# Softmax denominators one pair of heads later, in the form of the product with values, and the rotation split in keys and queries: a macaron block on one core

## What is computed

```python
x = x + 0.5 * ffn(layernorm(x))      # 2 shared and 8 routed experts, top 2
x = x + attn(layernorm(x))
x = x + 0.5 * ffn(layernorm(x))
```

```python
q = q * cos + rotate_half(q) * sin + fenc        # the same for k
dots = einsum('bhid,bhjd->bhij', q, k) * scale
attn = softmax(dots, axis=-1)
out = einsum('bhij,bhjd->bhid', attn, v)
return out @ w_out.T + b_out
```

## Time and profile before

| | |
|---|---|
| median of three runs | 1268.65 us (1264.79, 1268.65, 1268.78) |
| profiled execution, its own time | 1265.84 us |
| its span, first to last instruction | 1264.0 us |
| TensorE busy | 1224.8 us, 97% of the span |
| VectorE, GpSimd, ScalarE busy | 958.6, 897.0, 629.8 us |
| mean granted TensorE clock | 0.999 of 2.4 GHz |

### The profile page before, as it was taken

One profiled execution on the slowest core, in us unless ns is written; L12 is line 12 of the kernel. 1 busy time (PEld: TensorE's weight loads), 2 busy tenths in 40 slices (PEclk: granted clock), 3 DMA queues, 4 the chain that ended last, 5 costly groups with the idle time before them and its releaser, 6 DMA issues.

```text
span 1264.0 us, 20948 instructions
## 1 busy us (share of the span) xinstructions
PE 1224.8 (97%) x7346; PEld 777.6 (62%) x7346; DVE 958.6 (76%) x1439; ACT 629.8 (50%) x921; POOL 897.0 (71%) x652
## 2 busy tenths in 40 slices
PE   5999999899999999999999999999999999999998
PEld 3666666456666656565666666665666655666665
DVE  6666687778898888888888888788888766666632
ACT  3444532455555555546555555555555554434422
POOL 0444346688898999898889889889989862543443
PEclk9999999999999999999999999999999999999999
DMA  5351241123232323233332323232323221442140
GB/s 170 135 184 55 81 145 24 34 52 69 57 72 52 77 52 74 54 69 60 64 66 60 68 60 69 52 77 54 73 54 73 56 44 20 142 143 105 47 159 17
DMA packets 118677, 95.35 MB, mean 75 GB/s; under 512 B 75760, under 2 KB 85008, under 8 KB 118320
## 3 DMA queue, kind: packets, MB, share of 16 engines
q1 hardware_dynamic: 118064, 93.75, 30.0%
q10 hardware_dynamic: 512, 0.26, 0.1%
HBM read 57.53 MB, written 2.88 MB: 48 GB/s over the span
## 4 chain that ended last, share of the span: by engine, by line
PE 85%; DVE 6%; issue 4%; ACT 2%; POOL 2%; DMA 1%; SPq 0%; ACTq 0%; DVEq 0%; POOLq 0%
PE banks L1165 17%; PE banks L1144 14%; PE banks L455 12%; PE banks L468 8%; PE banks L1083 7%; PE banks L1003 6%; PE banks L1181 5%; PE banks L1149 4%; PE banks L1190 4%; PE banks L1011 3%; PE banks L1122 1%; DVE side_turned L702 1%; PE banks L410 1%; POOL work L1438 1%; PE banks L417 1%
## 5 line engine op out<-in xcount | busy, mean ns | idle before, releaser
L1015 DVE TENSOR_REDUCE neg_max<-banks 128x2 f32<-128x1024 f32 x256 | 305.3, 1226 | 12.7 <-PE banks L1003 7.7
L1267 ACT ACTIVATE work<-banks 128x1024 f32<-128x1024 f32 x256 | 262.5, 1027 | 92.7 <-PE banks L1149 76.6
L1165 PE MATMUL banks<-work 128*64 128x512 f32 x1024 | 233.8, 598 | 0.0
L1438 POOL TENSOR_TENSOR work<-work 128x1024 f32<-128x1024 f32 x64 | 158.8, 2482 | 74.2 <-PE banks L1165 74.2
L1428 POOL TENSOR_TENSOR turn<-turn,side_turned 128x512 f32<-128x512 f32 x128 | 164.9, 1311 | 30.7 <-DMA side_turned<-side 30.7
L1422 POOL TENSOR_TENSOR turn<-turn,fenc 128x512 f32<-128x512 f32 x128 | 163.3, 1298 | 2.0 <-DVE side L1338 2.0
L1433 POOL TENSOR_TENSOR qk_l<-turn,qk_h 128x512 fp32r<-128x512 f32 x128 | 162.1, 1289 | 2.1 <-ACT qk_h L992 2.1
L1165 PEld LDWEIGHTS banks<-work 128*64 128x64 f32 x1024 | 67.8, 136 | 132.7 <-issue 110.0
L1359 DVE TENSOR_TENSOR work<-work 128x1024 f32<-128x1024 f32 x64 | 107.4, 1677 | 37.7 <-PE banks L1165 37.5
L816 POOL TENSOR_TENSOR o_raw<-o_raw,work 128x512 f32<-128x512 f32 x52 | 67.2, 1293 | 88.0 <-DVE o_raw L734 80.7
L816 POOL TENSOR_TENSOR work<-work 128x512 f32<-128x512 f32 x44 | 56.6, 1297 | 96.0 <-DVE work L734 49.6
(11 more groups left out here) (178 smaller groups left out, 2454.7 us busy)
## 6 DMA issues: line engine op xcount, KB each, us to landing
work<-share SPq DMA_DIRECT2D x32, 1024.0 KB, 9.4
side_turned<-side SPq DMA_DIRECT2D x256, 128.0 KB, 3.1
rec_all<-rec_d SPq DMA_DIRECT2D x128, 128.0 KB, 2.9
x_tok<-in_x SPq DMA_DIRECT2D x8, 256.0 KB, 6.3
out<-x_tok SPq DMA_DIRECT2D x8, 256.0 KB, 9.4
work<-in_w_gate_up SPq DMA_DIRECT2D x1, 1280.0 KB, 6.7
work<-in_w_qk SPq DMA_DIRECT2D x1, 1024.0 KB, 11.8
den_d<-den_rows ACTq DMA_DIRECT2D x64, 4.0 KB
```

What stands on the lines that cost most here:

```text
L1015: return nc.vector.tensor_reduce(neg_max[:, g % 2, qt::DH], of, AX.X, ALU.max, negate=True)
L1165: ins = nc.tensor.matmul(o_bank(g)[OWN[h], :], v_all[:, kt, n * DH:(n + 1) * DH], pt[:, g % 2, kt, h * T:(h + 1) * T], start=(kt == 0), st ...
L1267: nc.scalar.activation(pt[:, g % 2, kt, :], S[kt].rearrange("p h q -> p (h q)"), ACT.Exp, scale=QSCALE).then_inc(s["probs"], 1)
L1438: nc.gpsimd.tensor_tensor(pt[:, g % 2, 2, :], pt[:, g % 2, 2, :], pt[:, g % 2, 3, :], ALU.add).then_inc(s["second_sum"], 1)
```

## The change

- The denominators of pair p-2, not p-1, are computed in period p, directly behind the product with values of pair p-1. They use the 128x64 form: one product per head and tile over all 512 queries, with ones of 64 columns, into bank 5 (the other bank of the even maxima) instead of bank 7.
- The product with values takes the key tiles in the order 2, 3, 0, 1. VectorE's sum is now of tiles 2 and 3 (`late_sum`), GpSimd's of tiles 0 and 1, written over tile 3 (`early_sum`, which also waits for `late_sum`).
- The output projection and all behind the denominators (reciprocals, normalise, residual) come one pair later; `o_raw` is three deep. The output projection stands ahead of the values on TensorE, and ScalarE's copy of the denominators stands behind `copy_o`, on 512 columns.
- `rope` is four instructions: keys, which wait for the keys' projection alone, then queries.
- In the tail, the reciprocals of pair 61 join those of pair 62, and there is one more output projection.

The diff, cut to its core:

```diff
+            ORDER = (2, 3, 0, 1)
+            def den_bank(g):
+                return bank[5] if own_bank(g + 1) else W
                 def project_both(g, p):
-                    project(g, K, KQ[:, K, :])
+                    project(g, K, KQ[:, K, :]).then_inc(s["k_ps"], 1)
                 def maxima(g, qt):
                     if qt == 1:
-                        at_least(pe, s["den_copied"], g - 2)
-                        at_least(pe, s["y_done"], g - 4)
+                        at_least(pe, s["den_copied"], g - 3)
+                        at_least(pe, s["y_done"], g - 5)
                 def denominators(g, p):
-                    pe.wait_ge(s["v_ready"], min(p + 4, B * 2 * TT))
+                    if den_bank(g) is W:
+                        pe.wait_ge(s["v_ready"], B * 2 * TT)
+                        pe.wait_ge(s["maxes"], N * TT)
                     at_least(pe, s["den_copied"], g)
-                    pe.wait_ge(s["first_sum"], g + 1)
-                    pe.wait_ge(s["second_sum"], g + 1)
-                    for n, kt in enumerate((0, 2)):
+                    pe.wait_ge(s["late_sum"], g + 1)
+                    pe.wait_ge(s["early_sum"], g + 1)
+                    for kt in (2, 3):
                         for h in range(2):
-                            for a in range(2):
-                                c, first = 32 * (2 * h + a), h * T + a * HALF
-                                ins = nc.tensor.matmul(W[c:c + 32, 0:HALF], ones_f[:],
-                                                       pt[:, g % 2, kt, first:first + HALF], start=(n == 0), stop=(n == 1))
+                            ins = nc.tensor.matmul(den_bank(g)[OWN[h], :], ones_f[:], pt[:, g % 2, kt, h * T:(h + 1) * T],
+                                                   start=(kt == 2), stop=(kt == 3))
...
                     if exists(last):
-                        for kt in range(TT):
+                        for kt in ORDER:
                             apply_v(last, kt)
+                    if exists(p - 2):
+                        denominators(p - 2, p)
                     if exists(nxt):
                         turn_maxima(nxt, p)
...
                         project_both(new, p)
+                    if exists(p - 4):
+                        project_out(p - 4, p)
                     if value_tile(p):
                         values(p)
-                    if exists(p - 3):
-                        project_out(p - 3, p)
...
-                    if exists(last) and p != JOIN_LOGITS_AT:
-                        denominators(last, p)
...
                 def copy_den(g):
-                    nc.scalar.activation(den_rows[:, 0:HALF], W[:, 0:HALF], ACT.Copy).then_inc(s["den_copied"], 1)
+                    nc.scalar.activation(den_rows[:], den_bank(g), ACT.Copy).then_inc(s["den_copied"], 1)
...
                     if exists(last):
                         copy_o(last)
+                    if exists(p - 2):
+                        copy_den(p - 2)
...
                 def rope(g):
-                    for to, part in ((turn[:, g % 2], 0), (side[:], 1)):
-                        ins = nc.vector.tensor_tensor(to, KQ, rope_t[:, part:part + 1, :].broadcast_to([P, QK, T]), ALU.mult)
+                    for part, done in ((K, s["k_ps"]), (Q, s["qk_ps"])):
+                        dve.wait_ge(done, g + 1)
+                        nc.vector.tensor_tensor(turn[:, g % 2, part], KQ[:, part, :], rope_t[:, 0, :], ALU.mult)
+                        ins = nc.vector.tensor_tensor(side[:, part], KQ[:, part, :], rope_t[:, 1, :], ALU.mult)
...
-                def second_sum(g):
+                def early_sum(g):
                     pool.wait_ge(s["o_ps"], g + 1)
-                    nc.gpsimd.tensor_tensor(pt[:, g % 2, 2, :], pt[:, g % 2, 2, :], pt[:, g % 2, 3, :],
-                                            ALU.add).then_inc(s["second_sum"], 1)
+                    pool.wait_ge(s["late_sum"], g + 1)
+                    nc.gpsimd.tensor_tensor(pt[:, g % 2, 3, :], pt[:, g % 2, 0, :], pt[:, g % 2, 1, :],
+                                            ALU.add).then_inc(s["early_sum"], 1)
...
                     ffn2["vector"](dve, "experts")
+                    reciprocals(N - 3)
                     reciprocals(N - 2)
                     ffn2["vector"](dve, "masks")
...
                 for p in PERIODS:
-                    if exists(p - 2):
-                        den_in(p - 2)
-                        reciprocals_out(p - 2)
-                        reciprocals_in(p - 2)
+                    if exists(p - 3):
+                        den_in(p - 3)
+                        reciprocals_out(p - 3)
+                        reciprocals_in(p - 3)
```

More of the change, by code:

```diff
@@ L164, in macaron @@
         ones_r = sb("ones_r", [P, P], F32R)
-        ones_f = sb("ones_f", [P, 32])
-        o_raw = sb("o_raw", [P, 2, T])
+        ones_f = sb("ones_f", [P, DH])
+        o_raw = sb("o_raw", [P, 3, T])
         den_rows = sb("den_rows", [P, T])
@@ L1246, in pe @@
                     ffn2["tensor"](pe, "turn")
-                    for kt in range(TT):
+                    for kt in ORDER:
                         apply_v(N - 1, kt)
                 elif tail == 0:
-                    project_out(N - 3, N)
+                    project_out(N - 4, N)
                 elif tail == 1:
                     denominators(N - 1, N)
+                elif tail == 3:
+                    project_out(N - 3, N)
                 elif tail == 5:
@@ L1265, in exponentials @@
                     if kt == 0:
+                        at_least(act, s["early_sum"], g - 1)
+                    if kt == 2:
                         at_least(act, s["den_ps"], g - 1)
@@ L1355, in reciprocals, with late_sum @@
                     nc.vector.reciprocal(rec_c[:, g % 2], den_c[:]).then_inc(s["rec_ready"], 1)
-                def first_sum(g):
-                    dve.wait_ge(s["first_applied"], g + 1)
-                    nc.vector.tensor_tensor(pt[:, g % 2, 0, :], pt[:, g % 2, 0, :], pt[:, g % 2, 1, :],
-                                            ALU.add).then_inc(s["first_sum"], 1)
+                def late_sum(g):
+                    dve.wait_ge(s["last_applied"], g + 1)
+                    nc.vector.tensor_tensor(pt[:, g % 2, 2, :], pt[:, g % 2, 2, :], pt[:, g % 2, 3, :],
+                                            ALU.add).then_inc(s["late_sum"], 1)
                 def residual(g):
@@ L1382, in period @@
                             maxima(nxt, qt)
-                    if exists(p - 2):
-                        reciprocals(p - 2)
+                    if exists(p - 3):
+                        reciprocals(p - 3)
                     end_norm(p)
@@ L1388, in period @@
                     if exists(p - 1):
-                        first_sum(p - 1)
+                        late_sum(p - 1)
                     if exists(nxt):
@@ L1397, in period @@
                         rope(new)
-                    if exists(p - 3):
-                        residual(p - 3)
+                    if exists(p - 4):
+                        residual(p - 4)
                 if tail is None:
@@ L1410, in dve @@
                 elif tail == 1:
+                    residual(N - 4)
+                elif tail == 4:
                     residual(N - 3)
-                elif tail == 4:
                     reciprocals(N - 1)
@@ L1459, in period @@
                         bias(p // PAIRS)
-                    if exists(p - 3):
-                        normalise(p - 3)
+                    if exists(p - 4):
+                        normalise(p - 4)
                     if exists(ahead):
@@ L1501, in pool @@
                     period(p)
+                normalise(N - 4)
+                early_sum(N - 1)
                 normalise(N - 3)
-                second_sum(N - 1)
                 normalise(N - 2)
@@ L1542, in sync @@
                 for p in PERIODS:
-                    if exists(p - 2):
-                        den_in(p - 2)
-                        reciprocals_out(p - 2)
-                        reciprocals_in(p - 2)
+                    if exists(p - 3):
+                        den_in(p - 3)
+                        reciprocals_out(p - 3)
+                        reciprocals_in(p - 3)
                     if exists(p + 3):
                         turn_partitions(p + 3)
-                den_in(N - 2)
-                reciprocals_out(N - 2)
-                reciprocals_in(N - 2)
+                for g in (N - 3, N - 2):
+                    den_in(g)
+                    reciprocals_out(g)
+                    reciprocals_in(g)
                 den_in(N - 1)
```

31 lines of the change are left out of this document (15 added, 16 removed).

## The result

The changed kernel took 1329.35 us (median of four runs, 1327.14 to 1332.17) against 1267.41 us for the kernel before in the same runs: a ratio of 1.0492, with a 95% interval of 1.0462 to 1.0523. It is slower by some 62 us. The profiled execution of the changed kernel took 1332.17 us, the slowest of the four, with a span of 1330.4 us at a mean granted clock of 0.994; its span is 66.4 us longer than the one the prediction reckoned from (1264.0).

A forecast was written before the change was run, and what follows sets the result against it. TensorE's own instructions, 85% of the chain, were taken to bound the kernel. The terms 40.3 - 2.3 + 5.6 + 5.5 + 7.1 = +56.2 us on 1265.84 gave 1322.0 us, range 1304 to 1337.

The forecast's parts named there:

- 64 pairs on TensorE: TensorE, every pair: denominators' new products add 1.72 us, their old place saves 1.09; net +0.63 each, +40.3 us.
- waits at the start: TensorE's two waits for GpSimd's sum disappear, as the sum is a period old when used: -2.3 us.
- second maxima product, 7 new batches: New batches' periods: x_high behind the denominators' copy delays rotation and residual; this product waits some 0.8 us, +5.6 us.
- first scores, 7 periods ahead of them: Period ahead of each new batch: ScalarE's four normalised tiles end later, so scores come 0.78 us later, +5.5 us.
- tail: Second FFN: VectorE stands 7.1 us at the second of two adjacent reciprocals, TensorE behind it; +7.1 us, 0 at least.
- The added step: TensorE behind the product with values: four products of 512 columns for the denominators, 1.72 us a pair.
- The saved step: TensorE between output projection and first maxima product: removing the old denominators saves 1.09 us a pair, bounds 1.00 to 1.18.
- The covers on VectorE: Plain periods: residual and first maximum end some 0.2 us before TensorE's second and third maxima products need their banks; no cost.
- (a): Rival: only TensorE's own price, covers hold everywhere; 38 us slower, 1304 us; chance 18%.
- (b): Rival: VectorE late, second and third maxima products wait about 0.3 us in some 50 plain periods; 1337 us; chance 11%.
- (c): Rival: TensorE follows a loop through the rotation, so earlier keys gain and added products fill idle time; 1241 us; 4%.
- (d): Rival: a late sum makes TensorE stand before the denominators; 0.3 us in 64 periods adds 19 us, 1341 us; 2%.

The follow-up runs named there:

- tail mended: Changed kernel with pair 61's reciprocals put ahead of the second FFN's routing steps: 1320.1 us, ratio 1.0422.
- the run with the form alone: Kernel before with only the denominators' form changed to two tiles of 64 columns, at their old place: 1319.34 us, ratio 1.0425.
- whole-rotation run: Changed kernel with the rotation back in two instructions over keys and queries: 1350.13 us, ratio 1.0658.
- either repair: Changed kernel with either pair 61's reciprocals ahead of the routing (1320.1 us), or ScalarE's x_high and normalised tiles moved ahead of its copies (1319.69 us).
- even with both: Changed kernel with pair 61's reciprocals ahead of the routing and ScalarE's two steps moved: 1310.96 us, ratio 1.0356.
- the split alone: Kernel before with only the rotation split into four instructions, keys then queries: 1265.03 us, ratio 0.9998.

## Why the prediction was right, and where its terms were off

The direction, the mechanism and the order of the terms held. The profiled difference of 66.4 us came out as follows, in the terms of the sum:

| term | forecast | measured |
|---|---|---|
| 64 pairs on TensorE | 40.3 (0.63 each) | 46.4 (0.725 each) |
| waits at the start | -2.3 | -3.1 |
| second maxima product, 7 new batches | 5.6 (0.8 each) | 5.5 (0.78 each) |
| first scores, 7 periods ahead of them | 5.5 (0.78 each) | 4.6 (0.65 each) |
| tail | 7.1 | 11.0 (8.3 standing, 2.7 at the lower clock) |
| lower clock in the first FFN, not the change's | none | 1.6 |
| sum | 56.2 | 66.0 |

0.4 us are not accounted for. The measured -3.1 is worked out from the transposes of the maxima. From that of period 0 to that of period 3 it is 36.42 us instead of 37.75; no denominators run in the first of these three stretches in either kernel, so the longer step would have added 2 x 0.725 = 1.45, and the gain is 2.8. Another 0.3 lie ahead of them: period 0's transpose is at 241.88 in the changed kernel with its tail mended and at 242.19 in the kernel before.

**The added step** was costed at 1.72 from eight products of the very sequence; it took 1.73. That half as many tiles take about twice as long is what the run with the form alone shows on its own, 1.00 to 1.86.

**The saved step** is the term of the main sum that was mis-sized: 1.00 instead of 1.09. The reading that failed is "left of it: the output projection followed by products of the same 128x128 form, 0.81". The 0.81 is right (652.37 to 653.18 above). But the first product behind the output projection then starts its successor 0.32 later (653.18 to 653.50) where products of the values follow each other at 0.23. The reading in the second FFN stopped at the first product behind the output projection; one row further the same 0.32 would have stood there (1083.59 to 1083.91 in the kernel before). The order that the change sets up carries that 0.09 in every pair, 5.8 us in 64. The lower bound given for the saving, 1.00, was the value. Both sets of products have the same form, so it isn't the change of form. The first product of the keys, behind the transpose of the maxima, shows it as well (613.65 to 613.97 above). In all three places the products behind have float32r operands and those ahead float32; that this is the cause fits, but no run tried it apart.

**The covers on VectorE** held where they were said to hold. The whole-rotation run measures the margin at 0.14 us where about 0.2 was given, and what stands behind it at 21 us. The Trainium skill's formula (VectorE: DVE Perf Modes, section on the TRN2 errata) put two more instructions at an estimated 0.31 us. The rows give less: from the rotation to the residual it is 654.37 - 651.97 = 2.40 in four instructions against 652.53 - 650.26 = 2.27 in two, so 0.13. The 0.70 that the keys' half was to start earlier is the longest of the waits in the earlier trace rows, which average 35.4 / 54 = 0.66; the rotation starts at 651.97, mark - 2.10, where it was forecast.

**ScalarE's two terms** came within 0.15 us of the forecast in each period, at the places named.

**The tail** was the right mechanism with two sizes missing. First, "a load lands in 1.84" left out that it has to be issued: from the issue at 1119.57 to the reciprocal it is 2.46, and the stretch before it 5.87 instead of 5.27. Standing 8.3 instead of 7.1 is that. Second, the lower clock behind a gap of that length, 2.7 us, was no term at all.

**The rivals.** (a), only TensorE's price: against it stand the runs with either repair; even with both, the kernel is 45.9 us over the kernel before, where that rival has 38: about the mis-sized saving (5.8) and what is left in the new batches' periods (7 x 0.32). (b), VectorE late in every period: the whole-rotation run shows what it would look like, 57 waits for the residual against 7. (c), the loop through the rotation: the split alone gave 0.9998. (d), late sums: no wait of TensorE for GpSimd's sum is left.

## What to carry to other kernels

Count how many tiles of a step run side by side, and over how many columns, before the changes of form around it: here the place behind a product of the same form was worth 0.145 us a pair, and the form it asked for cost 0.87. When a step is taken out of the bounding engine's stretch, ask what another engine did under it: a split that is worth nothing before can be what keeps the change from costing 21 us more. And when work moves by a period, walk through the fill and the drain as well as the steady state: two reciprocals that met behind the last period cost 11.0 us, a quarter of the 46.4 of the steady loss, and moving one line gave most of it back.

## What the runs showed of the hardware that was not expected

TensorE's granted clock fell while it stood for 9.17 us in the tail of the changed kernel: 0.58 on average in the 5 us before it started again, 0.50 (1.2 GHz) in the 5 us after, 0.90 in the next, then 1.00. The same products took 6.24 us against 3.50 in the kernel without the gap, so this wait cost some 30% more than its own length. The Trainium skill (TensorE: Matmul & The Clock Gate, Part 1) says that the throttled state is the default and activity releases it; the trace agrees.

Much shorter waits were followed by the lower level too, and not each time. In the profiled execution of the changed kernel, TensorE stood 1.22 us up to 33.52 and 0.45 us up to 34.27 in the first FFN, and the granted clock from 35 to 40 us was 0.66. In that of the kernel before, it stood 1.21 and 0.45 us up to the same points, and the clock stayed at 1.00. What decides it was not followed.

The first product of the values or of the gate starts its successor 0.32 us later, not 0.23, when it follows the output projection, and so does the first product of the keys behind the transpose of the maxima, though all of them have the 128x128 form.
